# Attention inside a transformer layer on eight cores: softmax reciprocals broadcast in f32 without a bf16 copy, and a barrier ahead of attention

## The chip, the cores and the metric

The kernel runs on all 8 cores of one Trainium2 chip, cores 0 to 3 on one die and 4 to 7 on the other. Each core works on one of the 8 sequences of the batch and on nothing else; the cores exchange no data. The metric is the device time of the slowest core in microseconds.

## The reference

One layer: attention with a residual on a layer-normed input, then a linear map with low-rank updates and a residual, also on a layer-normed input. Each core has 2048 tokens of width 4096, 32 query heads and 8 key/value heads of width 128.

```python
x = x + attn(layernorm(x), Wq, Wk, Wv, Wo, cos, sin)
x = x + ffn(layernorm(x), W, bias, A, Bf, coeffs, scales)

# attn: each key/value head serves 4 query heads
q = rope((x @ Wq).reshape(b, s, 32, 128)); k = rope(x @ Wk); v = x @ Wv
scores  = einsum('bhqd,bhkd->bhqk', q, k) / sqrt(128)      # causal mask
weights = softmax(scores)
ctx     = einsum('bhqk,bhkd->bhqd', weights, v)
return ctx @ Wo

# ffn
out = x @ W.T + bias
upd = sum_e coeffs[e] * scales[e] * (x @ A[e].T) @ Bf[e].T
```

## The kernel before

Five programs, one for each engine, are written out by hand. Every engine runs its instructions in order; a helper `INC` counts a semaphore up when an instruction ends, `wge` makes an engine wait for a count, `W` makes one named engine wait for all counted so far. `bar` drains all engines and makes each wait for the others.

The stages run in this order, all with the width on the partitions and the tokens in the free dimension: constants (`p0`); for each half H of 1024 tokens a layer norm (`p_ln`), the projections of q, k and v (`p2`) and attention of that half's queries over all keys so far (`p3`); then the output projection (`p4`), two layer norms and the second linear map (`p6`). Before, there is a barrier after each `p3` and none between `p2` and `p3`.

`p2` makes 48 outputs of 128 rows: 32 q heads, spilled to memory as bf16 (`q_spill`), 8 k heads and 8 v heads kept on chip. For each q and k head it also finds the largest squared norm (L401, into `BND`). The k heads end before the v heads begin. In the v part TensorE transposes (L502) and ScalarE copies (L508) while VectorE has nothing left of `p2`.

`p3` first turns the norms into one bound for all scores: VectorE does 8 copies or maxima (L545, L547), 32 products (L553) and a reduction (L557) on single elements, ScalarE a root and a sign (L565, L567), TensorE a broadcast (L573), ScalarE a copy into `NEGB` (L579). Then it runs 32 blocks, for 16 pairs of heads and two groups jj of 512 queries. A block has `kcn` chunks of 128 keys: 4 and 8 in half 0, 12 and 16 in half 1, and the last four of each are masked. Per chunk, TensorE computes the scores of both heads (L681, L683), VectorE adds the mask where there is one (L702, L704), ScalarE takes the exponential into bf16 (L716), and TensorE adds the chunk to the denominators with a matrix of ones (L734, L735, PSUM columns 3072 to 4095) and to the context (L737, L738, PSUM columns 2048 to 3071). Scores run two chunks ahead.

At a block's end ScalarE copies the raw context out (L750, L751), and VectorE takes the reciprocals of the two denominators on one partition (L759, L760) into `ROWS` in f32, then casts both (L762, L763) into one row of `SQS` or `OSTG` in bf16. The context is scaled one block later by the tail: after the first two chunks' scores of block idx, the tail of block idx-2 is emitted. In it TensorE broadcasts the two reciprocals over 128 partitions into PSUM 2048 to 3071 (L605, L607), and VectorE copies these to `RBS` (L620, L621) and multiplies the context (L624, L625). In half 0 the result then goes to memory (L633, L635). VectorE's order at a block's start is thus: reciprocals and casts of block idx-1, tail of block idx-2, masks of block idx. TensorE's first L734 of a block waits for the casts of block idx-1, the context copies of block idx-1 and the `RBS` copies of block idx-2.

GpSimd loads each block's q (L658, L659) two blocks ahead. In either half the first two blocks' loads need only the first two spills of q and are issued once GpSimd has done its weight loads of `p2`. The f32 matrix of ones `ONESF`, one row of 128, is also used by `p_ln`, which broadcasts rows of f32 with it (L310 to L313).

Of the kernel before, what the change touches and what calls it, by code (L numbers as in the profile page):

```python
# [40 lines left out]
class B:  # L41
# [109 lines left out]
    def emit(self, me, eng):  # L151
        self.me = me
        self.eng = eng
        self.C = {k: 0 for k in SEM_NAMES}

        self.p0()
        self.bar()
        for H in (0, 1):
            self.p_ln(self.x_fm, lambda kc: self.arena(self.U1, kc), H,
                      dbg=self.dbg_ln1 if self.debug else None)  # L160
            if self.upto >= 2:
                self.p2(H)
            if self.upto >= 3:
                self.p3(H)
                self.bar()
            else:
                self.bar()
        if self.upto >= 2 and self.debug:
            self.p2_dbg()
            self.bar()  # L170
        if self.upto >= 4:
            self.p4()
            self.bar()
        if self.upto >= 5:
            for H in (0, 1):
                U = self.U1 if H == 0 else self.U2
                self.p_ln(self.xprime, lambda kc, U=U: self.arena(U, kc), H,
                          dbg=self.dbg_ln2 if self.debug else None)
        if self.upto >= 6:
            self.p6()  # L180
        self.bar()
        if self.on("sync"):
            self.eng.wait_ge(self.sems["out0"], self.C["out0"])
            self.eng.wait_ge(self.sems["out1"], self.C["out1"])
            self.eng.wait_ge(self.sems["dbg"], self.C["dbg"])
# [345 lines left out]
    def p3(self, H):  # L531
        on, INC = self.on, self.INC
        eng = self.eng
        PS, SCB, Q3, MSK, RBS = self.PS, self.SCB, self.Q3, self.MSK, self.RBS
        BND, NEGB, ROWS = self.BND, self.NEGB, self.ROWS
        RCB = self.SQS

        self.W("vector", "nrm")
        if on("vector"):
            self.wge("qsp", self.C["qsp"])  # L540
            i = None
            for kv in range(NKV):
                kslot = 64 + kv * 2 + H
# [47 lines left out]
        sc_tot = []  # L591
        pends = []

        def rcb_row(g, head):
            t = self.SQS if g % 2 == 0 else self.OSTG
            return t[0:1, head * 512:(head + 1) * 512]

        def emit_tail_pe(g):
            gi, h0, h1, jj = g
            if on("tensor"):  # L600
                self.wge("rc", base_rc + 2 * (gi + 1))
                self.wge("cev", base_cev + min(2 * (gi + 2), 2 * NH))
                if gi >= 1:
                    self.wge("rbe", base_rbe + 2 * gi)
                INC(eng.matmul(PS[:, 2048:2560], self.ONESR[0:1, :], rcb_row(gi, 0),  # L605
                               start=True, stop=True), "rb", 1)
                INC(eng.matmul(PS[:, 2560:3072], self.ONESR[0:1, :], rcb_row(gi, 1),  # L607
                               start=True, stop=True), "rb", 1)
            else:
                INC(None, "rb", 1)  # L610
                INC(None, "rb", 1)
# [30 lines left out]
        for hp in range(NH // 2):  # L642
            kv = hp // 2
            h0, h1 = 2 * hp, 2 * hp + 1
            for jj in range(2):
# [7 lines left out]
                if on("gpsimd"):  # L653
                    if idx >= 2:
                        self.wge("sc", sc_tot[idx - 2])
                    else:
                        self.wge("qsp", self.C["qsp"] - 16 * 30)
                    INC(eng.dma_start(qs0, self.q_spill[h0, :, q0:q0 + 512]), sq, 16)  # L658
                    INC(eng.dma_start(qs1, self.q_spill[h1, :, q0:q0 + 512]), sq, 16)  # L659
                else:  # L660
                    INC(None, sq, 16)
                    INC(None, sq, 16)
# [9 lines left out]
                def emit_scores(kc):  # L672
                    if on("tensor"):
                        if kc == 0:
                            self.wge(sq, base_q[p] + 32 * (idx // 2 + 1))
                            if idx == 0:
                                self.wge("ev2", self.C["ev2"])
                        if kc >= 2:
                            self.wge("exp", base_exp + (kc - 1))
                        lhsT = self.kfm(kv)[:, kc * 128:(kc + 1) * 128]  # L680
# [15 lines left out]
                for kc in range(kcn):  # L696
# [24 lines left out]
                    if on("tensor"):  # L721
                        self.wge("exp", base_exp + (kc + 1))
                        if kc == 0:
                            self.wge("rc", base_rc + 2 * idx)
                            self.wge("cev", base_cev + 2 * idx)
                            if idx >= 1:
                                self.wge("rbe", base_rbe + 2 * (idx - 1))
                            else:
                                self.wge("vev", self.C["vev"])
                                self.wge("nrm", self.C["nrm"])  # L730
                        st, sp = (kc == 0), (kc == kcn - 1)
                        e0 = SCB[:, (kc % 2) * 1024:(kc % 2) * 1024 + 512]
                        e1 = SCB[:, (kc % 2) * 1024 + 512:(kc % 2 + 1) * 1024]
# [18 lines left out]
                else:  # L752
                    INC(None, "cev", 1)
                    INC(None, "cev", 1)
                rc0 = ROWS[0:1, 0:512]
                rc1 = ROWS[0:1, 512:1024]
                if on("vector"):
                    self.wge("vdn", base_vdn + 2 * kcn)
                    INC(eng.reciprocal(rc0, PS[0:1, 3072:3584]), "chn", 1)  # L759
                    INC(eng.reciprocal(rc1, PS[0:1, 3584:4096]), "chn", 1)  # L760
                    self.wge("chn", self.C["chn"])
                    INC(eng.tensor_copy(rcb_row(idx, 0), rc0), "rc", 1)  # L762
                    INC(eng.tensor_copy(rcb_row(idx, 1), rc1), "rc", 1)  # L763
                else:
                    INC(None, "chn", 1)
                    INC(None, "chn", 1)
                    INC(None, "rc", 1)
                    INC(None, "rc", 1)
                pends.append((idx, h0, h1, jj))
# [260 lines left out]
```

## Time and profile before

| | us |
|---|---|
| median of 2 runs | 6090.76 |
| lowest and highest | 6077.15, 6104.36 |
| the profiled execution | 6069.31 |
| its span, slowest core (core 3) | 6067.8 |
| spans of the other cores | 6022.6 to 6056.3 |
| attention of half 0, half 1 on core 3, about | 727, 1073 |

The span is the time from the first to the last instruction of a core. All rows are of core 3. TensorE is busy for 77% of the span, VectorE for 33%, ScalarE for 21%. A line like L605 is line 605 of the kernel before. In a timeline, a matmul's start is measured and its end modelled: two matmuls that follow each other at the full clock start 0.22 us apart although each is shown with 0.38 us. The granted clock is that of TensorE, as a share of 2.4 GHz.

### The profile page before, as it was taken

Reading aid. Unit: us, or ns where it says so; the run is one execution under the profiler, and the core shown is the slowest. Engines: PE = TensorE matmul, PEld = TensorE weight load, DVE = VectorE, ACT = ScalarE, POOL = GpSimd, SP = SyncE. Lnnn points to the kernel's source line nnn. Section 1 sums busy time; section 2 is a strip of 40 time slices with the busy share of each in tenths; the row PEclk is TensorE's granted clock in tenths of the full one; section 3 lists DMA queues with packets and bytes.
Section 4 is the critical chain, followed back from the end, with each engine's and each line's share of the span. In section 5 each row is a group of like instructions: output and inputs, shape, how many; then the busy total and the mean of one; then the engine's idle time right before and its main releaser. Section 6 shows DMA issues by size and latency. Waiting matters only on the chain.

```text
span 6067.8 us, 50466 instructions; the slowest of 8 cores (6022.6 to 6067.8 us)
## 1 busy us (share of the span) xinstructions
PE 4660.8 (77%) x19656; PEld 1911.8 (32%) x19656; DVE 2019.1 (33%) x2001; ACT 1264.8 (21%) x1352; POOL 384.7 (6%) x366
## 2 busy tenths in 40 slices
PE   3399997454442999986666765899999446999999
PEld 0134443111110444432222222344444102444444
DVE  0644531666625454404444343000000172000000
ACT  4011112333332111124544544000000440000000
POOL 0001110000000111100000001000000000000000
PEclk6699998787765999998888888899999557999999
DMA  6278863000041888730000001666665532666665
GB/s 143 26 75 92 91 66 37 23 25 23 25 92 42 87 89 94 72 40 7 9 7 9 7 9 31 124 117 113 116 114 108 142 101 26 112 110 113 109 107 103
DMA packets 758102, 429.63 MB, mean 71 GB/s; under 512 B 685760, under 2 KB 693984, under 8 KB 757616
## 3 DMA queue, kind: packets, MB, share of 16 engines
q0 software_dynamic: 684144, 199.88, 32.8%
q1 hardware_dynamic: 73728, 226.53, 11.9%
q8 instruction: 164, 2.69, 0.2%
q14 instruction: 66, 0.54, 0.0%
HBM read 506.56 MB, written 92.27 MB: 99 GB/s over the span
## 4 chain that ended last, share of the span: by engine, by line
PE 67%; DVE 17%; DMA 8%; ACT 5%; issue 2%; POOL 0%; ACTq 0%; DVEq 0%; SPq 0%; POOLq 0%
PE PS L423 10%; PE PS L424 10%; PE PS L942 7%; PE PS L829 7%; PE PS L943 7%; PE PS L830 7%; DVE ROWS L759 4%; DVE ROWS L760 3%; PE PS L734 3%; DMA XST<-x_fm 3%; ACT SCB L716 2%; DMA WS<-wq 2%; PE PS L735 2%; PE PS L737 2%; DMA XST<-xprime 2%
## 5 line engine op out<-in xcount | busy, mean ns | idle before, releaser
L423 PE MATMUL PS<-U,WS 128*128 128x512 bf16 x3072 | 1180.1, 384 | 177.2 <-DVE U L333 150.7
L424 PE MATMUL PS<-U,WS 128*128 128x512 bf16 x3072 | 1178.5, 384 | 0.0
L716 ACT ACTIVATE SCB<-PS,NEGB 128x1024 bf16<-128x1024 f32 x640 | 708.5, 1116 | 919.8 <-PE PS L683 507.2
L829 PE MATMUL PS<-U,WS 128*128 128x512 bf16 x2048 | 777.7, 380 | 48.2 <-DMA WS<-wo 48.2
L942 PE MATMUL PS<-U,WS 128*128 128x512 bf16 x2048 | 777.7, 380 | 20.0 <-DMA BFT<-bf_r 20.0
L734 PE MATMUL PS<-SCB,ONES 128*128 128x512 bf16 x640 | 271.6, 424 | 678.2 <-ACT SCB L716 343.1
L943 PE MATMUL PS<-U,WS 128*128 128x512 bf16 x2048 | 777.7, 380 | 0.0
L830 PE MATMUL PS<-U,WS 128*128 128x512 bf16 x2048 | 777.6, 380 | 0.0
L702 DVE TENSOR_TENSOR PS<-PS,MSK 128x512 f32<-128x512 f32 x256 | 178.7, 698 | 971.2 <-PE PS L683 968.7
L423 PEld LDWEIGHTS PS<-U,WS 128*128 128x128 bf16 x3072 | 303.6, 99 | 577.4 <-issue 232.1
L424 PEld LDWEIGHTS PS<-U,WS 128*128 128x128 bf16 x3072 | 303.6, 99 | 360.3 <-issue 15.9
L260 ACT CAST U<-XST 128x1024 bf16<-128x1024 f32 x128 | 133.6, 1044 | 1158.3 <-DMA XST<-xprime 1022.4
L973 DVE SCALAR_TENSOR_TENSOR U<-PS,BIAS,XST 128x1024 f32<-128x1024 f32 x64 | 82.1, 1283 | 878.9 <-PE PS L953 713.6
L734 PEld LDWEIGHTS PS<-SCB,ONES 128*128 128x128 bf16 x640 | 66.1, 103 | 943.4 <-issue 942.3
L848 DVE TENSOR_TENSOR U<-PS,XST 128x1024 f32<-128x1024 f32 x64 | 78.4, 1225 | 855.5 <-PE PS L830 829.0
L829 PEld LDWEIGHTS PS<-U,WS 128*128 128x128 bf16 x2048 | 200.7, 98 | 291.6 <-issue 50.8
L401 DVE TENSOR_REDUCE BND<-PS 1x1 f32<-1x1024 f32 x80 | 97.0, 1212 | 584.2 <-PE PS L395 584.2
L942 PEld LDWEIGHTS PS<-U,WS 128*128 128x128 bf16 x2048 | 200.7, 98 | 262.9 <-issue 22.1
L943 PEld LDWEIGHTS PS<-U,WS 128*128 128x128 bf16 x2048 | 200.7, 98 | 242.5 <-issue 1.7
L830 PEld LDWEIGHTS PS<-U,WS 128*128 128x128 bf16 x2048 | 200.7, 98 | 242.4 <-issue 1.6
L460 ACT ACTIVATE OSTG<-XST 128x1024 bf16<-128x1024 f32 x64 | 67.6, 1057 | 987.1 <-DVE XST L446 987.1
L735 PE MATMUL PS<-SCB,ONES 128*128 128x512 bf16 x640 | 269.0, 420 | 0.0
(135 smaller groups left out, 4647.6 us busy)
## 6 DMA issues: line engine op xcount, KB each, us to landing
XST<-x_fm SPq DMA_DIRECT2D x128, 512.0 KB, 4.7
WS<-wq POOLq DMA_DIRECT2D x64, 1024.0 KB, 13.5
XST<-xprime SPq DMA_DIRECT2D x128, 512.0 KB, 4.3
WS<-wo POOLq DMA_DIRECT2D x32, 1024.0 KB, 16.1
xprime<-U SPq DMA_DIRECT2D x64, 512.0 KB, 3.5
WS<-wf POOLq DMA_DIRECT2D x32, 1024.0 KB, 16.9
out_fm<-U SPq DMA_DIRECT2D x64, 512.0 KB, 3.6
q_spill<-OSTG SPq DMA_DIRECT2D x64, 256.0 KB, 5.3
```

The lines of the kernel that those rows point to most:

```text
L423: eng.matmul(region[:, 0:512], lhsT, ln[:, 0:512], start=st, stop=sp)
L424: mmi = eng.matmul(region[:, 512:1024], lhsT, ln[:, 512:1024], start=st, stop=sp)
L702: eng.tensor_add(region(kc)[:, 0:512], region(kc)[:, 0:512], MSK[:, mi, :])
L716: INC(eng.activation(SCB[:, (kc % 2) * 1024:(kc % 2 + 1) * 1024], region(kc), AF.Exp, bias=NEGB[:, 0:1], scale=1.0), "exp", 1)
L734: eng.matmul(PS[:, 3072:3584], self.ONES2[:, :], e0, start=st, stop=sp)
L735: eng.matmul(PS[:, 3584:4096], self.ONES2[:, :], e1, start=st, stop=sp)
L759: INC(eng.reciprocal(rc0, PS[0:1, 3072:3584]), "chn", 1)
L760: INC(eng.reciprocal(rc1, PS[0:1, 3584:4096]), "chn", 1)
L829: eng.matmul(region[:, 0:512], lhsT, rhs[:, 0:512], start=st, stop=sp)
L830: mmi = eng.matmul(region[:, 512:1024], lhsT, rhs[:, 512:1024], start=st, stop=sp)
L942: eng.matmul(region[:, 0:512], lhsT, rhs[:, 0:512], start=st, stop=False)
L943: eng.matmul(region[:, 512:1024], lhsT, rhs[:, 512:1024], start=st, stop=False)
```

## The change

The two casts L762 and L763 go, with the wait between them and the reciprocals. The reciprocals of a block are written to one half of `ROWS`, by the block's parity, and the tail's broadcasts read them from there as f32, with `ONESF` in place of the bf16 ones `ONESR`. As a row of `ROWS` is used again two blocks later, the reciprocals of block idx wait for the broadcasts of block idx-2. A barrier of all engines comes between `p2` and `p3` in both halves. With it, the waits at the start of `p3` for q spills (`qsp`), rope results (`ev2`), v copies (`vev`) and norms (`nrm`) are taken out.

```diff
             if self.upto >= 2:
                 self.p2(H)
+            self.bar()
             if self.upto >= 3:
                 self.p3(H)
-                self.bar()
-            else:
                 self.bar()
...
         self.W("vector", "nrm")
         if on("vector"):
-            self.wge("qsp", self.C["qsp"])
...
-        def rcb_row(g, head):
-            t = self.SQS if g % 2 == 0 else self.OSTG
-            return t[0:1, head * 512:(head + 1) * 512]
+        def rec_row(g, head):
+            return ROWS[0:1, (g % 2) * 1024 + head * 512:(g % 2) * 1024 + (head + 1) * 512]
...
-                INC(eng.matmul(PS[:, 2048:2560], self.ONESR[0:1, :], rcb_row(gi, 0),
+                INC(eng.matmul(PS[:, 2048:2560], self.ONESF[0:1, :], rec_row(gi, 0),
                                start=True, stop=True), "rb", 1)
-                INC(eng.matmul(PS[:, 2560:3072], self.ONESR[0:1, :], rcb_row(gi, 1),
+                INC(eng.matmul(PS[:, 2560:3072], self.ONESF[0:1, :], rec_row(gi, 1),
                                start=True, stop=True), "rb", 1)
...
                     if idx >= 2:
                         self.wge("sc", sc_tot[idx - 2])
-                    else:
-                        self.wge("qsp", self.C["qsp"] - 16 * 30)
                     INC(eng.dma_start(qs0, self.q_spill[h0, :, q0:q0 + 512]), sq, 16)
...
-                            if idx == 0:
-                                self.wge("ev2", self.C["ev2"])
...
-                            else:
-                                self.wge("vev", self.C["vev"])
-                                self.wge("nrm", self.C["nrm"])
...
-                rc0 = ROWS[0:1, 0:512]
-                rc1 = ROWS[0:1, 512:1024]
                 if on("vector"):
                     self.wge("vdn", base_vdn + 2 * kcn)
-                    INC(eng.reciprocal(rc0, PS[0:1, 3072:3584]), "chn", 1)
-                    INC(eng.reciprocal(rc1, PS[0:1, 3584:4096]), "chn", 1)
-                    self.wge("chn", self.C["chn"])
-                    INC(eng.tensor_copy(rcb_row(idx, 0), rc0), "rc", 1)
-                    INC(eng.tensor_copy(rcb_row(idx, 1), rc1), "rc", 1)
+                    if idx >= 2:
+                        self.wge("rb", base_rb + 2 * (idx - 1))
+                    INC(eng.reciprocal(rec_row(idx, 0), PS[0:1, 3072:3584]), "rc", 1)
+                    INC(eng.reciprocal(rec_row(idx, 1), PS[0:1, 3584:4096]), "rc", 1)
```

## Rows read from the trace of the kernel before

**Rows 1.** Windows, the two attention stretches: length, then each engine's busy us, PEclk.

```profile
1009.00:1736.00 727.00, 350.63 (x1216) 119.26 (x1216) 458.46 (x510) 246.15 (x257) 31.96 (x60) 0.79 0.07 22
2702.00:3775.00 1073.00, 718.64 (x2752) 255.32 (x2752) 462.54 (x512) 528.26 (x513) 31.98 (x60) 0.87 0.02 8
```

**Rows 2.** Waits, whole span: who waited for whom, us, times, longest us.

```profile
PE PS L734 <- ACT SCB L716: 343.1, 196, 10.9
PE PS L734 <- DVE RBS L621: 307.9, 45, 7.0
```

**Rows 3.** Timeline of one block boundary: start us, us, instruction, idle before and releaser.

```profile
1114.10 3.35 DVE L759 RECIPROCAL ROWS<-PS 1x512 f32<-1x512 f32 x1 [2.54 <-PE PS L738]
...
1115.40 0.37 PE L605 MATMUL PS<-OSTG,ONESR 1*128 1x512 bf16 x1 [0.55 <-ACT U L751]
...
1115.62 0.37 PE L607 MATMUL PS<-OSTG,ONESR 1*128 1x512 bf16 x1
1117.37 3.28 DVE L760 RECIPROCAL ROWS<-PS 1x512 f32<-1x512 f32 x1
...
1121.43 0.67 DVE L620 CAST RBS<-PS 128x512 bf16<-128x512 f32 x1
...
1122.85 0.59 PE L734 MATMUL PS<-SCB,ONES 128*128 128x512 bf16 x1 [6.86 <-DVE RBS L621]
```

**Rows 4.** Groups by line, whole span, half of the casts: busy us, mean ns.

```profile
L762 DVE CAST SQS<-ROWS 1x512 bf16<-1x512 f32 x32 | 13.3, 415 | 3.3
L763 DVE CAST SQS<-ROWS 1x512 bf16<-1x512 f32 x32 | 13.0, 408 | 0.0
```

**Rows 5.** Timeline of the first layer norm: from the third broadcast to its reader.

```profile
166.61 1.91 PE L312 MATMUL PS<-XST,ONESF 1*128 1x512 f32 x2
...
170.32 1.01 ACT L319 COPY MR<-PS 128x1024 f32<-128x1024 f32 x1 [14.04 <-PE PS L313]
```

**Rows 6.** Timeline of the end of half 0: the last tail.

```profile
1734.04 0.58 PE L605 MATMUL PS<-OSTG,ONESR 1*128 1x512 bf16 x1 [6.44 <-DVE RBS L621]
...
1735.22 0.69 DVE L620 CAST RBS<-PS 128x512 bf16<-128x512 f32 x1 [0.40 <-PE PS L607]
```

**Rows 7.** Timeline of half 0: the softmax bound, from VectorE to the first scores.

```profile
869.44 0.56 DVE L545 COPY BND<-BND 1x1 f32<-1x1 f32 x8 [0.17 <-DVE BND L401]
...
872.52 0.17 DVE L557 TENSOR_REDUCE BND<-BND 1x1 f32<-1x32 f32 x1
...
1007.28 0.20 ACT L565 ACTIVATE BND<-BND 1x1 f32<-1x1 f32 x1
...
1009.07 0.59 PE L681 MATMUL PS<-Q,U 128*128 128x512 bf16 x1 [0.61 <-ACT NEGB L579]
```

**Rows 8.** Timeline across the barrier behind half 1.

```profile
3774.68 0.42 DVE L625 TENSOR_TENSOR U<-U,RBS 128x512 bf16<-128x512 bf16 x1
3775.28 0.33 SPq L839 DMA_DIRECT2D XST<-x_fm  x1
3775.74 0.54 POOL L801 DMA_DIRECT2D U<-ctx_sp  x1 [82.55 <-ACTq L138]
```

**Rows 9.** The line L659, the second q load of a block.

```profile
DMA to landing us min/median/max: 2.4/2.5/11.4
```

**Rows 10.** Groups by line, window of half 0, then of half 1: first scores matmul.

```profile
L681 PE MATMUL PS<-Q,U 128*128 128x512 bf16 x192 | 83.9, 437 | 0.6 <-ACT NEGB L579 0.6
...
L681 PE MATMUL PS<-Q,U 128*128 128x512 bf16 x448 | 182.6, 408 | 0.6 <-ACT NEGB L579 0.6
```

**Rows 11.** Timeline of TensorE in the q projection of half 0, behind two gaps.

```profile
277.57 0.38 PE L423 MATMUL PS<-U,WS 128*128 128x512 bf16 x1 [2.15 <-DMA WS<-wq]
...
297.32 0.59 PE L423 MATMUL PS<-U,WS 128*128 128x512 bf16 x1 [5.25 <-DVE MR L442]
297.70 0.63 PE L424 MATMUL PS<-U,WS 128*128 128x512 bf16 x1
...
303.24 0.40 PE L423 MATMUL PS<-U,WS 128*128 128x512 bf16 x1
```

More of the change, by code:

```diff
@@ L535, in p3 @@
         BND, NEGB, ROWS = self.BND, self.NEGB, self.ROWS
-        RCB = self.SQS
         self.W("vector", "nrm")
         if on("vector"):
-            self.wge("qsp", self.C["qsp"])
             i = None
@@ L754, in p3 @@
                     INC(None, "cev", 1)
-                rc0 = ROWS[0:1, 0:512]
-                rc1 = ROWS[0:1, 512:1024]
                 if on("vector"):
                     self.wge("vdn", base_vdn + 2 * kcn)
-                    INC(eng.reciprocal(rc0, PS[0:1, 3072:3584]), "chn", 1)
-                    INC(eng.reciprocal(rc1, PS[0:1, 3584:4096]), "chn", 1)
-                    self.wge("chn", self.C["chn"])
-                    INC(eng.tensor_copy(rcb_row(idx, 0), rc0), "rc", 1)
-                    INC(eng.tensor_copy(rcb_row(idx, 1), rc1), "rc", 1)
-                else:
-                    INC(None, "chn", 1)
-                    INC(None, "chn", 1)
+                    if idx >= 2:
+                        self.wge("rb", base_rb + 2 * (idx - 1))
+                    INC(eng.reciprocal(rec_row(idx, 0), PS[0:1, 3072:3584]), "rc", 1)
+                    INC(eng.reciprocal(rec_row(idx, 1), PS[0:1, 3584:4096]), "rc", 1)
+                else:
                     INC(None, "rc", 1)
```

## The prediction, made before the changed kernel was run

> **What bounds the kernel now.** I read the cores' spans first, then the windows, the waits, the groups by line, and last the timeline around single block boundaries. The change lies in the two attention halves, so only these matter. The windows [rows 1] give 727 us for half 0 and 1073 us for half 1. No engine is busy all the time in either: TensorE 351 and 719 us, VectorE 458 and 463 us, ScalarE 246 and 528 us, at a granted clock of 0.79 and 0.87. What sets the time is what TensorE waits for. The waits [rows 2] show two large ones ahead of L734, the first matmul on a fresh exponential: 343.1 us for ScalarE, 307.9 us for VectorE's L621, the latter in 45 waits of up to 7.0 us.
>
> The timeline of one boundary [rows 3] shows what L621 stands for. When a block's last matmul ends, VectorE starts two one-row reciprocals (3.35 and 3.28 us), then two one-row casts of their results (L762, L763), then the two evictions L620 and L621 that belong to the block before. Only then may TensorE overwrite the PSUM these read (L734 at 1122.85). TensorE's own part, the broadcast L605/L607, starts at 1115.40 and is over some 7 us before. So VectorE's chain is the path at the boundary. In the blocks that begin with masked chunks the release comes through the mask adds and an exponential, but these too queue on VectorE behind the same chain. There are 32 blocks in each half, 64 boundaries with the two half ends.
>
> **The change, part by part.**
>
> *The casts go.* Each is 415 and 408 ns [rows 4], on one partition; they overlap a little with their neighbours, so I take starts from the timeline [rows 3]. From L760's start (1117.37) to L620's start (1121.43) is 4.06 us. L760 takes 3.28 us, and without casts L620 could start about 3.21 us after it starts (an engine's next instruction starts here some 0.07 us before the record of the last one ends, as L760 follows L759: 1114.10 + 3.35 against 1117.37 leaves 0.08). Gain 4.06 - 3.21 = 0.85 us a boundary, 64 x 0.85 = 54 us. Nothing else covers it: TensorE is idle throughout.
>
> *The broadcasts read f32.* Attention shows none at this width; the layer norm does: two f32 broadcasts of one row of 512 (L312, L313, at the low clock) take from 166.61 to ScalarE's start at 170.32, 3.71 us [rows 5]. The bf16 pair starts 0.22 us apart at the full clock [rows 3]. As upper bound of the f32 pair I take 3.71 us, as lower bound the bf16 pair's 0.6 us; likely is about half the upper one, 1.9 us, since the clock is full there. At a boundary the pair starts at 1115.40 and would end by 1119.1 at worst; VectorE is in its reciprocals until 1120.6, so it costs nothing, with 1.5 us to spare. It starts when ScalarE's L751 ends, which is tied to the same last matmul as the reciprocals, so the margin is the same in every block. The new wait of the reciprocals on `rb` is for a broadcast issued a whole block earlier and is met. The Trainium skill, "FP8 and Floating Point Precision", section "TensorE Precision Notes", says that true FP32 takes four passes through the array; by it the pair would be 8 x 0.22 = 1.8 us at the full clock, and hidden as well.
>
> At each half's end the cover is gone: the last tail starts when VectorE is done and all wait for it. There the bf16 pair takes from 1734.04 to L620 at 1735.22, 1.18 us [rows 6], and the f32 pair at the low clock 3.71 us: +2.5 us, twice, +5 us.
>
> *The barrier before attention.* Now VectorE's work for the softmax bound runs during the V projection: 869.44 to 872.69, 3.25 us [rows 7], over 130 us before it is needed. Behind a barrier it comes after the last V copy. A barrier costs 0.2 to 0.6 us from the last engine's end to the others' next issue [rows 8]; I take 0.25. Then 3.25 us, one handover of 0.1, and the rest of the chain as before (L565 at 1007.28 to L681 at 1009.07, 1.79 us). Added: 3.6 us a half, +7 us. The first q loads, until now issued ahead, start behind the barrier too: POOL at 0.65 us after the last engine's end [rows 8], two issues of 0.54, landing 2.5 us after the second issue starts [rows 9]: about 3.7 to 4.2 us, against 5.4 us of the bound chain, hidden. Queued behind these on POOL are only later q loads. The waits taken out cost nothing by themselves; SP's `qsp` wait at the end of the projection is for spills long landed.
>
> *Sum.* -54 + 5 + 7 = -42 us against the profiled execution's 6069.3 us: 6027. That execution is 21.5 us below the median of the runs, 6090.8 us; so -42 us from there, 6049 us.
>
> **What the clock may do.** It is the largest unknown. Each block begins at the low clock: L681's mean is 437 ns in half 0 and 408 in half 1 [rows 10]. A matmul's record is 0.38 us at the full clock and 0.63 at the low one [rows 11]. So (437 - 380)/250 = 23% of the 1152 matmuls of half 0 and 11% of the 2688 of half 1 ran low (the other five lines of a chunk lie near L681), 560 in all, nearly 9 a block. Low ones start 0.42 us apart (14 of them from 297.32 to 303.24 [rows 11]), full ones 0.22: 0.21 us lost each, about 118 us in all. The change shortens TensorE's idle gap before L734: from 6.86 us by 0.85 and by 1.3 for the longer broadcast, to about 4.7 us. Would the clock then stay up? In the projection a gap of 2.15 us left the matmul after it at 0.38; one of 5.25 us was followed by 14 low ones [rows 11]. 4.7 us is nearer to the second, so I take no gain, and keep -118 us as the bound below. The bound above: if every block had the 14 low matmuls of that case instead of 9, 5 x 0.21 x 64 = +67 us.
>
> **The rivals.**
>
> *Clock held.* If the shorter gap keeps the full clock in every block: -42 - 118 = -160 us, 5931 us, 2.6% faster; in half of them 5990. For it: the gap shrinks by a third. Against it: the 5.25 us case, and gaps of the masked blocks, which are longer. The Trainium skill, "TensorE: Matmul & The Clock Gate", section "HAM oscillation", says that waits between bursts of matmuls make each burst start at the low clock, and only long ones do; by it shortening a gap can pay more than its own length. The low starts here agree with it.
>
> *Longer low spells.* The instants at which the level changes are not tied to the blocks, so a shift of the blocks may lengthen them; at the bound -42 + 67 = +25, 6116 us, slower than before. It decides from 42/(0.21 x 64) = 3 more low matmuls in a block on average. For it: spells of 14 occur. Against it: nothing selects the long ones.
>
> *f32 broadcasts not hidden.* They must take over 5.2 us a pair (1115.40 to 1120.6). At twice the layer norm's 3.71 us, 2.2 us more in 62 blocks: -42 + 136 + 7 = +101 us, 6192 us. The row speaks against it.
>
> *q loads late.* The longest landing is 11.4 us [rows 9], beside weight loads: 0.65 + 0.54 + 11.4 - 5.4 = 7 us a half, +14: 6063 us. No weights are in flight behind the barrier.
>
> *The change doesn't pay.* If the blocks were paced by something else and the casts only filled a wait, -54 falls away: +12 us, 6103 us. The chain of [rows 3], without a gap on VectorE, speaks against it.
>
> **How the numbers follow.** Forecast 0.68; q late 0.10; longer low spells 0.08; doesn't pay 0.06; clock held 0.06; not hidden 0.02. Predicted: 6049 us, 0.7% below before. The range of 6005 to 6100 takes in the forecast with the executions' own scatter (6077 to 6104 us before), q late, half of the clock's bounds and most of the case of no gain. What this kernel's measurement can tell from no change is 2%, 122 us. Faster by more: the clock held in most blocks, 0.05. Slower by more: 0.02. Within: 0.93.
>
> **What would show it.** No L762/L763; L620 about 3.2 us after L760's start; TensorE's gap before L734 about 4.7 us; f32 broadcasts of some 1.9 us a pair that end before L620 starts, half 0 near 703 us and half 1 near 1048 us, each from its first scores; VectorE's bound work between the last V copy and the first scores, 3.6 us. L681's mean near 437 and 408 would confirm that the clock is unchanged. Wrong would be: L620 waiting for a broadcast, or these means well off.

## The result and the profile after

| | before | after |
|---|---|---|
| executions, us, without the disturbed | 6070.5 to 6104.4 (8) | 6031.1 to 6060.9 (10) |
| ratio of the two | | 0.9932, 95% interval 0.9915 to 0.9949 |
| profiled execution, its span, us | 6069.3, 6067.8 | 6034.8, 6033.2 |
| last V transpose to first scores | 2.4 | 5.9 |
| half 0, first scores to last scaling | 729.5 | 716.7 |
| half 1 | 1073.8 | 1045.7 |
| low matmuls in half 0, half 1 | 284, 339 | 341.5, 328.5 |

The change makes the kernel 0.7% faster, some 41 us of 6080. (About half of all executions, of either kernel, were disturbed on one die or both and took 3 to 12% longer; with them the median before is 6180.87 us and after 6047.87, a difference that the change did not make.) The last four lines are medians over the cores whose matmul records are complete, worked out from the trace. A low matmul is one of the six chunk lines whose record is over 0.5 us; the total is 1152 in half 0 and 2688 in half 1. These four numbers are the yardstick for everything below: what lies ahead of the first scores alone differs by 23 to 33 us between the cores of one execution (they start at 976 to 1009 us before, at 984 to 1007 after), the halves by 1 to 3.

In the code after, the reciprocals are L748 and L749, the broadcasts L601 and L603, the evictions L616 and L617, and the first matmul on a fresh exponential L723. The same windows as [rows 1], on the slowest core (length, then busy us of TensorE, weight loads, VectorE, ScalarE and GpSimd, each with its count, granted clock, DMA share, GB/s):

```profile
1006.00:1725.00 719.00, 408.60 (x1282) 141.12 (x1282) 433.71 (x448) 246.45 (x259) 32.07 (x60) 0.80 0.07 23
2685.00:3732.00 1047.00, 757.35 (x2818) 273.36 (x2818) 436.73 (x448) 528.49 (x515) 32.07 (x60) 0.89 0.03 8
```

VectorE has 62 and 64 instructions and some 25 us less in a half: the casts. TensorE has 66 records and 58 and 39 us more: some 45 us a half are the longer f32 broadcasts, which run where it would be idle, the rest in half 0 is longer records of chunk matmuls. The halves are shorter by 8 and 26 us in these rough cuts, by 12.8 and 28.1 us when measured from first scores to last scaling. The two halves did not gain alike. The waits (who waited for whom, us, times, longest) beside [rows 2]:

```profile
PE PS L723 <- ACT SCB L708: 306.4, 197, 8.4
PE PS L723 <- DVE RBS L617: 208.4, 45, 4.7
```

The wait for the evictions is 99.5 us shorter, though only 54 us of casts went: 45 such waits shrink by 0.85 us for the casts, and by some 1.3 us that the longer broadcasts now fill (97 us in all), and the second part gains nothing. Ahead of the blocks of 4 chunks, which begin with a masked one, TensorE's wait is longer in both kernels, 10.5 us before and 8.3 after. One block boundary, beside [rows 3] (timeline, core 1: start, us, instruction, idle before it and its releaser):

```profile
2822.85 3.35 DVE L748 RECIPROCAL ROWS<-PS 1x512 f32<-1x512 f32 x1 [2.60 <-PE PS L727]
...
2824.09 1.09 PE L601 MATMUL PS<-ROWS,ONESF 1*128 1x512 f32 x2 [0.55 <-ACT U L740]
...
2825.02 1.02 PE L603 MATMUL PS<-ROWS,ONESF 1*128 1x512 f32 x2
...
2826.12 3.28 DVE L749 RECIPROCAL ROWS<-PS 1x512 f32<-1x512 f32 x1
2829.33 0.61 DVE L616 CAST RBS<-PS 128x512 bf16<-128x512 f32 x1
2829.88 0.66 DVE L617 CAST RBS<-PS 128x512 bf16<-128x512 f32 x1
...
2830.69 0.58 PE L723 MATMUL PS<-SCB,ONES 128*128 128x512 bf16 x1 [4.65 <-DVE RBS L617]
```

From L749's start to L616's it is 3.21 us, against 4.06 in [rows 3]. The f32 broadcasts take 1.95 us together and are over 3.3 us before L616 starts. L616 waits for nothing: VectorE's chain from L748 to L723 is still the path. It is 7.84 us now, and was 8.75.

The start of half 0, beside [rows 7] (timeline, slowest core): the bound work has moved behind the barrier.

```profile
1001.56 0.50 ACT L507 CAST U<-PS 128x128 bf16<-128x128 f32 x2 [0.30 <-PE PS L501]
1002.30 0.56 DVE L542 COPY BND<-BND 1x1 f32<-1x1 f32 x8 [139.95 <-ACTq L138]
1002.71 0.57 POOL L652 DMA_DIRECT2D Q<-q_spill  x1 [41.05 <-ACTq L138]
...
1005.38 0.17 DVE L554 TENSOR_REDUCE BND<-BND 1x1 f32<-1x32 f32 x1
...
1007.34 0.59 PE L673 MATMUL PS<-Q,U 128*128 128x512 bf16 x1 [0.50 <-ACT NEGB L576]
```

The barrier itself costs 0.24 us from ScalarE's last copy (1002.06) to VectorE's first one; then come 3.25 us of scalar work on one element, L542 to L554, that [rows 7] shows 130 us earlier. TensorE is released by the bound (L576), not by the q load, which was issued at 1002.71.

The end of half 0, beside [rows 6] (timeline, core 3), where nothing lies beside the broadcasts:

```profile
1708.53 2.04 PE L601 MATMUL PS<-ROWS,ONESF 1*128 1x512 f32 x2 [3.72 <-DVE RBS L617]
...
1710.37 1.91 PE L603 MATMUL PS<-ROWS,ONESF 1*128 1x512 f32 x2
...
1712.80 0.69 DVE L616 CAST RBS<-PS 128x512 bf16<-128x512 f32 x1 [3.49 <-PE PS L603]
```

From L601 to L616 it is 4.27 us at the low clock, against 1.18 before: +3.1 us. At the end of half 1 it is 3.92 (3720.00 to 3723.92), +2.7.

Last the clock, by the mean record of a chunk's lines in half 0. The scores line of before is in [rows 10], 437 ns; its context line (groups by line, core 3, busy us and mean ns):

```profile
L737 PE MATMUL PS<-SCB,U 128*128 128x512 bf16 x192 | 83.4, 434 | 0.0
```

and the two lines after, on the slowest core:

```profile
L673 PE MATMUL PS<-Q,U 128*128 128x512 bf16 x192 | 85.3, 444 | 0.5 <-ACT NEGB L576 0.5
L726 PE MATMUL PS<-SCB,U 128*128 128x512 bf16 x192 | 88.8, 463 | 0.0
```

The scores matmul hardly shows it (437 to 444), the context matmul does (434 to 463): more of half 0 runs at the low clock than before.

### The profile page after: what moved, and what is told of

Read it like the earlier page. It is cut to its first block, busy times and chain, and to the rows that moved or that the text cites. A ratio compares the mean times of both kernels' runs of the same rounds, so it can differ in the third digit from the quotient of the medians.

```text
span 6033.2 us, 50608 instructions; the slowest of 8 cores (6005.6 to 6033.2 us)
## 1 busy us (share of the span) xinstructions
PE 4755.1 (79%) x19784; PEld 1950.1 (32%) x19784; DVE 1967.2 (33%) x1873; ACT 1264.5 (21%) x1352; POOL 385.4 (6%) x366
## 3 DMA queue, kind: packets, MB, share of 16 engines
q1 hardware_dynamic: 73728, 226.53, 12.8%
## 4 chain that ended last, share of the span: by engine, by line
PE 66%; DVE 13%; DMA 9%; ACT 6%; issue 5%; POOL 0%; ACTq 0%; DVEq 0%; SPq 0%; POOLq 0%
PE PS L422 10%; PE PS L423 10%; PE PS L813 7%; PE PS L814 7%; PE PS L926 7%; PE PS L927 7%; DVE ROWS L748 3%; PE PS L723 3%; DMA WS<-wq 3%; DMA XST<-x_fm 3%; ACT SCB L708 3%; DMA XST<-xprime 2%; PE PS L724 2%; PE PS L726 2%; PE PS L727 2%
## 5 line engine op out<-in xcount | busy, mean ns | idle before, releaser
L723 PE MATMUL PS<-SCB,ONES 128*128 128x512 bf16 x640 | 270.7, 423 | 548.1 <-ACT SCB L708 306.4
L723 PEld LDWEIGHTS PS<-SCB,ONES 128*128 128x128 bf16 x640 | 66.0, 103 | 828.8 <-issue 827.7
```

What stands on the lines that cost most here:

```text
L723: eng.matmul(PS[:, 3072:3584], self.ONES2[:, :], e0, start=st, stop=sp)
```

## The experiments

All are changes to the kernel after, except e2 and e7, which change the kernel before. All compute the whole reference. This table has the yardstick for each; the expectations stand as written before each ran. "Chain" is the time from the first reciprocal's start to the first eviction's start at a boundary, against before.

| kernel | chain | gap | half 0 | half 1 | low, half 0 | low, half 1 | ratio to before (95%) |
|---|---|---|---|---|---|---|---|
| before | 0 | 2.4 | 729.5 | 1073.8 | 284 | 339 | 1 |
| after | -0.85 | 5.9 | 716.7 | 1045.7 | 341.5 | 328.5 | 0.9932 (0.9915 to 0.9949) |
| e1, no barrier | -0.85 | 2.4 | 716.1 | 1046.4 | 336 | 333 | 0.9959 (0.9914 to 1.0003) |
| e2, barrier alone | 0 | 6.1 | 731.0 | 1072.5 | 294 | 341.5 | 1.0054 (1.0013 to 1.0096) |
| e3, bf16 reciprocal | -0.85 | 6.0 | 714.0 | 1043.4 | 342 | 330 | 0.9966 (0.9927 to 1.0005) |
| e4, more broadcasts | -0.85 | 5.9 | 724.9 | 1100.5 | 338 | 326 | 1.0046 (1.0014 to 1.0078) |
| e7, casts twice | +0.68 | 2.5 | 762.7 | 1098.9 | 339.5 | 353 | 1.0107 (1.0049 to 1.0165) |
| e11, one copy | -0.24 | 6.1 | 726.9 | 1065.6 | 296 | 339 | none |
| e8, filled gap | -0.85 | 6.0 | 708.7 | 991.8 | 344.5 | 69 | 0.983 |
| e5, direct reciprocal | | 5.9 | 679.3 | 1005.6 | 375 | 312.5 | 0.9792 (0.9746 to 0.9839) |
| e6, denominators out | | 6.0 | 605.9 | 809.2 | 350.5 | 14 | 0.943 |
| e10, mask by matmul | | 6.1 | 389.6 | 765.6 | 10.5 | 13.5 | 0.892 |

Gap, halves and counts are as in the first table. Ratios without an interval rest on one or two executions.

**e1, no barrier.** The waits at the start of attention come back for the barrier, with two differences: GpSimd's is for all spills of q and not the first two, and VectorE's for the spills stays out. The rest of the change stays.

```
-            self.bar()
...
+                    else:
+                        self.wge("qsp", self.C["qsp"])
...
+                            if idx == 0:
+                                self.wge("ev2", self.C["ev2"])
...
+                            else:
+                                self.wge("vev", self.C["vev"])
+                                self.wge("nrm", self.C["nrm"])
```

> The changed kernel without its new barrier, with the waits at the start of attention put back; casts gone and f32 broadcasts as in the changed kernel. Chain theory (the time is VectorE's chain at each block boundary, the barrier only uncovers the bound's work): first scores about 2.5 us after the last V transpose instead of 6.0, halves unchanged at 717 and 1046 us, so some 7 us less than the changed kernel, ratio to before about 0.992. Rival (the barrier shifts the blocks and is what took back the missing 12 us of half 0): half 0 falls to about 705 us, ratio about 0.990.

Measured: the gap is back at 2.4 us and the halves are those of after, 716.1 and 1046.4 us. So the barrier costs 3.5 us a half ahead of the first scores, and changes nothing inside. Its 7 us are too few for the ratio: the intervals of e1 and after overlap.

**e2, barrier alone.** The kernel before with the barrier added, its precise waits kept.

```
+            self.bar()
```

> The kernel before with a barrier added between projection and attention, all else unchanged, casts and bf16 broadcasts kept. Chain theory: first scores 6.0 instead of 2.5 us after the last V transpose, halves unchanged at 729 and 1073 us, +7 us in all, ratio 1.001. Rival (the barrier disturbs more, by q loads that start late or by projection weights that come later): first scores over 8 us after the last transpose or another stage longer, ratio over 1.003.

Measured: the gap grows to 6.1 us, the halves stay (731.0 and 1072.5). The ratio, 1.0054, is more than the 7 us (0.1%) explain; in the profiled execution the excess lies in the projections of half 0 on cores 4 and 5, whose first scores start at 1053 and 1059 us, against 983 and 976 before (the granted clock in these projections is 0.90 on core 5 and 0.98 on core 1). The barrier comes behind these projections. The two runs give the barrier nearly the same price from both sides, 3.5 to 3.9 us a half.

**e3, bf16 reciprocal.** The reciprocal writes the bf16 row itself, so the casts are gone and the broadcasts are bf16, as before.

```
         def rec_row(g, head):
-            return ROWS[0:1, (g % 2) * 1024 + head * 512:(g % 2) * 1024 + (head + 1) * 512]
+            t = self.SQS if g % 2 == 0 else self.OSTG
+            return t[0:1, head * 512:(head + 1) * 512]
...
-                INC(eng.matmul(PS[:, 2048:2560], self.ONESF[0:1, :], rec_row(gi, 0),
+                INC(eng.matmul(PS[:, 2048:2560], self.ONESR[0:1, :], rec_row(gi, 0),
...
```

> The changed kernel with the reciprocals written as bf16 rows and broadcast by the bf16 ones: casts gone as in the change, but broadcasts as short as before; the barrier stays. Chain theory: VectorE's chain is as in the changed kernel, so half 1 stays near 1046 us and each half ends 2.5 us sooner; TensorE's gap before the first denominator matmul is about 6.0 instead of 4.7 us. Clock theory for half 0 (the missing 12 us are low-clock matmuls, set by where the blocks fall): the number of low matmuls in half 0 moves with the gap or not, and half 0's time moves by 0.21 us for each. Rival (the f32 broadcasts themselves cost in half 0): half 0 near 704 us with an unchanged number of low matmuls.

Measured: halves of 714.0 and 1043.4 us, 2.7 and 2.3 below after, all of it at the half ends. The period of a block of 4, 8, 12 and 16 chunks is 16.62, 27.68, 29.55 and 35.20 us, against 16.62, 27.67, 29.53 and 35.20 after. Inside the blocks the f32 broadcasts cost nothing. The low matmuls are those of after (342 and 330), with TensorE idle for 1.3 us longer at each boundary: what broadcasts fill of the gap makes no difference to the clock.

**e4, more broadcasts.** Three more f32 one-row matmuls at each boundary, to see when the cover ends and whether work on one row holds the clock.

```
+                for rep in range(2):
+                    eng.matmul(PS[:, 2048:2560], self.ONESF[0:1, :], rec_row(gi, 0),
+                               start=True, stop=True)
+                eng.matmul(PS[:, 2560:3072], self.ONESF[0:1, :], rec_row(gi, 1),
+                           start=True, stop=True)
```

> The changed kernel with three more f32 broadcasts in each tail, repeats of the same two into the same place, so that TensorE's idle gap before the first denominator matmul falls from about 4.7 to about 2.1 us in three of four blocks; VectorE's chain is the same. If one-row matmuls hold the clock up: low matmuls fall from about 340 and 320 to under 150 in each half, and some 60 to 100 us go, ratio about 0.980. If the clock doesn't count them or the gap is still too long: low matmuls and halves as in the changed kernel, ratio 0.993. If a tail starts at the low clock it takes 8.5 us, longer than its cover of 5.2: then up to 3 us more in such a block.

Measured: half 0 +8.2 us, half 1 +54.8 us against after. The low matmuls hardly move (338 and 326). The block periods in half 0 are those of after (16.64 and 27.65 us), and 5.1 of its 8.2 us are the last tail, which has no cover; in half 1 they grow by 1.8 and 1.3 us. One boundary of half 1 tells why (timeline, core 4; the first row holds two instructions):

```profile
2795.22 3.35 DVE L753 RECIPROCAL ROWS<-PS 1x512 f32<-1x512 f32 x1 [2.61 <-PE PS L732]
...
2796.46 1.95 PE L602 MATMUL PS<-ROWS,ONESF 1*128 1x512 f32 x4 [0.55 <-ACT U L745]
2798.25 1.60 PE L604 MATMUL PS<-ROWS,ONESF 1*128 1x512 f32 x2
2798.49 3.28 DVE L754 RECIPROCAL ROWS<-PS 1x512 f32<-1x512 f32 x1
2799.65 1.91 PE L606 MATMUL PS<-ROWS,ONESF 1*128 1x512 f32 x2
2801.35 1.91 PE L608 MATMUL PS<-ROWS,ONESF 1*128 1x512 f32 x2
2803.44 0.69 DVE L621 CAST RBS<-PS 128x512 bf16<-128x512 f32 x1 [1.66 <-PE PS L608]
```

TensorE works without a pause from 2796.46, and still its instructions go from 1.02 us to 1.91: the clock fell to its lower level (1.2 GHz) while TensorE ran one-row matmuls back to back; the granted clock is 1.00 in the 6 us before them and 0.65 over them. With that five of them outlast VectorE's reciprocals, and L621 waits 1.66 us for L608. In half 0 the last of them are shorter (L608 takes 1.4 us on average, 2.1 in half 1), and L621 waits 3.7 us for them in all, against 57.5 in half 1. This is the rival "f32 broadcasts not hidden", made to happen: it needs 2.5 times the work of the change.

**e7, casts twice.** The kernel before, with each cast done twice: two more casts in the chain.

```
+                    eng.tensor_copy(self.WS[0:1, 0, 0:4, :], rc0)
+                    eng.tensor_copy(self.WS[0:1, 0, 4:8, :], rc1)
                     INC(eng.tensor_copy(rcb_row(idx, 0), rc0), "rc", 1)
                     INC(eng.tensor_copy(rcb_row(idx, 1), rc1), "rc", 1)
```

> The kernel before with two more one-row casts at each block's end, the same as L762 and L763 but into an unused place; no barrier. Chain theory: VectorE's chain is 0.68 us longer at each of 64 boundaries, +43 us if the low-clock matmuls stay at 282 and 335 a half; each one more or fewer moves that by 0.21 us. Both halves' block periods grow by 0.68 us on average before that. Rival (part of the casts is covered, as half 0's gain of 12 instead of 24 us would say): half 0 grows by about half of 22 us with an unchanged number of low matmuls.

Measured: the two extra casts take 0.68 us from start to start. The halves grow by 33.2 and 25.1 us. 32 x 0.68 = 21.8 us of each is the chain. The rest, 11.4 and 3.3, is again low matmuls: 55.5 and 14 more, at 0.21 us 11.7 and 2.9. A longer chain also raises the count in half 0. The rival, casts that are partly covered, would have had half 0 grow by 11 us.

**e11, one copy.** The kernel after, with one one-row copy ahead of its reciprocals, so that the chain lies between that of after and that of before.

```
+                    eng.tensor_copy(self.SQS[0:1, (idx % 2) * 512:(idx % 2) * 512 + 512],
+                                    PS[0:1, 3072:3584])
                     INC(eng.reciprocal(rec_row(idx, 0), PS[0:1, 3072:3584]), "rc", 1)
```

> The changed kernel with one more VectorE instruction ahead of each block's reciprocals, a one-row copy of 512 out of PSUM into an unused place, some 0.60 us. VectorE's chain is then 0.25 us shorter than before the change, where the changed kernel's is 0.85 us shorter. Chain theory with the clock: half 0 takes 729 - 32 x 0.25 + 2.5 = 723.5 us plus 0.21 us for each low matmul above 283, half 1 1073.5 - 8 + 2.5 = 1068 us plus 0.21 us for each above 337; each within 3 us. The counts themselves are not foretold, except that they need not lie between those of the two kernels. Rival (half 0's missing 12 us is a cost that grows evenly with the chain): half 0 about 14 us over the changed kernel's, 731, whatever the counts.

Measured on core 1 alone, since in the only execution cores 2 and 3 took 2.7 times as long for half 0 and 3.7 times for half 1 (26 ms in all), and cores 4 to 7 took some 150 us longer outside the halves. Its chain is 0.24 us shorter than before's: 7.09 us (2852.84 to 2859.93) against 7.33 in [rows 3]. Half 0 is 726.9 us with 296 low matmuls, half 1 1065.6 with 339. The same row of arithmetic: 729.5 - 32 x 0.24 + 2.5 + 12 x 0.21 = 726.8; for half 1 it gives 1068.6, 3 us too much. So a quarter of the shortening brings a fifth of the additional low matmuls; but three other cores of that execution with whole records have 276, 306 and 279, as wide as before's own 281 to 299, so that the count did not clearly rise here.

**e8, filled gap.** The kernel e3, with 18 full-height bf16 matmuls (K as stationary, q as moving operand, results unused) ahead of the broadcasts at each boundary.

```
+                if fill is not None:
+                    for r in range(18):
+                        c = 2048 + (r % 2) * 512
+                        eng.matmul(PS[:, c:c + 512], fill[0], fill[1], start=True, stop=True)
```

> The changed kernel with bf16 reciprocals and bf16 broadcasts, and ahead of the two broadcasts of each tail 18 more matmuls of full height, 128x512 bf16, whose results nobody reads; they fill TensorE's idle time while VectorE takes the reciprocals. VectorE's chain is the same. Clock theory: matmuls of full height hold the clock where one-row matmuls did not; in three of four blocks TensorE then idles under 2.5 us. Low matmuls fall from about 340 and 327 to under 150 and 80; at 0.21 us each some 80 to 100 us go, ratio about 0.980. Rival (the low clock costs nothing, since ScalarE or VectorE paces those chunks): fewer low matmuls, but halves within 10 us of 714 and 1043.

Measured: half 1 falls from e3's 1043.4 to 991.8 us and its low matmuls from 330 to 69, half 0 from 714.0 to 708.7 with the count unchanged in the median (344.5, the cores from 278 to 382). Window of half 1 on core 1, after first, then e8:

```profile
2680.00:3727.00 1047.00, 749.23 (x2785) 270.41 (x2782) 436.77 (x448) 520.55 (x507) 42.72 (x81) 0.89 0.04 11
```

```profile
2692.00:3684.00 992.00, 769.48 (x3275) 288.59 (x3273) 436.67 (x448) 523.82 (x509) 40.77 (x77) 0.98 0.03 11
```

The granted clock is 0.98 instead of 0.89. TensorE does 540 useless matmuls more and is done sooner. Against e3, which has the same chain, it is 51.6 us for 261 low matmuls fewer, 0.20 us each. This settles the price of a low matmul, and that the clock, not only the chain, sets the time in half 1.

The filling is not the same in half 0. It takes 4 us of each wait and leaves 1.9 to 2.0 us ahead of blocks of 8, 12 and 16 chunks, but 5.7 us ahead of every block of 4, where the first mask adds and an exponential follow VectorE's chain. Two boundaries of half 0 (timeline, core 1):

```profile
1106.99 0.38 PE L729 MATMUL PS<-SCB,ONES 128*128 128x512 bf16 x1 [1.82 <-DVE RBS L623]
...
1134.08 0.59 PE L729 MATMUL PS<-SCB,ONES 128*128 128x512 bf16 x1 [5.69 <-ACT SCB L714]
```

By blocks the low matmuls of half 0 go from 10.9 to 7.3 in a block of 8 and from 10.1 to 13.8 in a block of 4, so the two cancel. Why those of 4 have more than without the filling is not explained.

**e5, direct reciprocal.** The ones matrix already leaves the denominators on all 128 partitions, so the reciprocal can be taken there, and broadcast and eviction go.

```
-                    INC(eng.reciprocal(rec_row(idx, 0), PS[0:1, 3072:3584]), "rc", 1)
-                    INC(eng.reciprocal(rec_row(idx, 1), PS[0:1, 3584:4096]), "rc", 1)
+                    self.wge("nmm", self.C["nmm"])
+                    INC(eng.reciprocal(RBS[:, 0, :], PS[:, 3072:3584]), "rc", 1)
+                    INC(eng.reciprocal(RBS[:, 1, :], PS[:, 3584:4096]), "rc", 1)
```

> The denominators already stand on all 128 partitions, as they come from a matrix of ones. This kernel takes the reciprocals there (128x512 in place of 1x512), into RBS as bf16, and multiplies the same block's context at once: no casts, no broadcasts, no RBS copies; barrier as in the changed kernel. If a reciprocal costs by its row length alone (3.3 us as on one partition), VectorE's chain ahead of the first denominator matmul loses the two RBS copies, 1.27 us a boundary: 64 x 1.27 = 81 us less than the changed kernel, and each half's end is shorter by about 5 us; ratio about 0.978, give or take 0.21 us for each low matmul more or less. If it costs more on 128 partitions, no gain.

Measured: 0.9792, halves of 679.3 and 1005.6 us. One boundary (timeline, core 1):

```profile
2791.10 3.36 DVE L717 RECIPROCAL RBS<-PS 128x512 bf16<-128x512 f32 x1 [2.61 <-PE PS L697]
...
2794.38 3.29 DVE L718 RECIPROCAL RBS<-PS 128x512 bf16<-128x512 f32 x1
...
2797.92 0.58 PE L693 MATMUL PS<-SCB,ONES 128*128 128x512 bf16 x1 [6.13 <-DVE RBS L718]
```

A reciprocal of 128 rows of 512 costs 3.36 us, of one row 3.35. The chain to the first matmul is 6.82 us against 7.84 after: 1.02 us a boundary (1.27 expected), 33 us a half, and the tail at the half end (6.5 us) is gone. That is 39 us; measured are 37.4 and 40.1, with 33 more low matmuls in half 0 (+7 us) and 16 fewer in half 1 (-3). With these the sum is 32 and 42 us, so it misses half 0 by 5 us and half 1 by 2.

**e6, denominators out.** The denominators are copied out of PSUM to SBUF at once, so that PSUM is free after two copies, and the reciprocals run under the next block.

```
+                INC(eng.reciprocal(RBS[:, head, :], dn), "rbe", 1)
...
-                    INC(eng.reciprocal(rec_row(idx, 0), PS[0:1, 3072:3584]), "rc", 1)
-                    INC(eng.reciprocal(rec_row(idx, 1), PS[0:1, 3584:4096]), "rc", 1)
...
+                    INC(eng.tensor_copy(DEN[:, dp:dp + 512], PS[:, 3072:3584]), "rc", 1)
+                    INC(eng.tensor_copy(DEN[:, dp + 512:dp + 1024], PS[:, 3584:4096]), "rc", 1)
```

> The reciprocals leave the path: at a block's end VectorE only copies the denominators of all partitions to SBUF (two copies of 128x512, 1.3 us), so that TensorE may go on; the reciprocals (128x512, bf16 out) and the context's scaling follow while the next block runs, ahead of its masks in blocks of 8 to 16 chunks and between the masks in those of 4. Chain theory: TensorE's wait falls from about 7.5 us after its last matmul to about 2.7, some 5 us less in 48 blocks and 1 to 2 in 16, 250 to 270 us; with the short gap the low matmuls of the 48 blocks go too, up to 100 us more. Ratio 0.940 to 0.955. Rival (something else paces the blocks): under 100 us.

Measured: halves of 605.9 and 809.2 us, an execution of 5734 us. One boundary (timeline, core 0):

```profile
2807.51 0.69 DVE L731 COPY XST<-PS 128x512 f32<-128x512 f32 x1 [2.61 <-PE PS L710]
...
2808.11 0.68 DVE L732 COPY XST<-PS 128x512 f32<-128x512 f32 x1
...
2808.97 3.35 DVE L604 RECIPROCAL RBS<-XST 128x512 bf16<-128x512 f32 x1 [0.17 <-DVE XST L732]
2809.87 0.38 PE L706 MATMUL PS<-SCB,ONES 128*128 128x512 bf16 x1 [1.68 <-ACT SCB L693]
```

The reciprocal is still there and as long as ever, but the next matmul starts 0.90 us into it: 2.36 us after the chain's start instead of 7.84. TensorE now waits for the exponential (L693), and only 14 of half 1's matmuls are low. In half 1, 5.48 x 32 = 175 us and 314 x 0.21 = 66 us make 241 us; measured are 236.5 less than after. In half 0 it is 111 us less, 3.5 a boundary, with as many low matmuls as ever (350.5). There TensorE still waits 3.4 us ahead of a block of 4 chunks and 4.0 us inside each block: the masks share VectorE with the reciprocals, which led to e10.

**e10, mask by matmul.** On top of e6 the causal mask is added by TensorE, in bf16 and with the identity, into the PSUM of the scores, instead of by eight VectorE operations a block. The reciprocals now stand ahead of the chunks in every block; in e6 they stood between the masks in blocks of 4.

```
+                        if kc >= diag0:
...
+                            eng.matmul(region(kc)[:, 0:512], lhsT, qs0, start=True, stop=False)
+                            eng.matmul(region(kc)[:, 512:1024], lhsT, qs1, start=True, stop=False)
+                            INC(eng.matmul(region(kc)[:, 0:512], idb, mk,
+                                           start=False, stop=True), "sc", 1)
+                            INC(eng.matmul(region(kc)[:, 512:1024], idb, mk,
+                                           start=False, stop=True), "sc", 1)
...
-                    isdiag = kc >= diag0
+                    isdiag = False
```

> As the kernel whose denominators are copied out, and the causal mask is added by TensorE, a matmul of a bf16 unit matrix with the mask into the scores, instead of by VectorE (L702, L704 before). The two mask adds of 0.69 us on VectorE and one handover go from each masked chunk's path, for two matmuls of 0.22 us. Half 0 is 605 us and half 1 809 us without this. If VectorE paces half 0's blocks (masks and reciprocals share it, 14 us of work in a block of 15): half 0 falls by 90 to 150 us, half 1 by 60 to 100 us (4 chunks of 2 us more each in 32 blocks, down to the plain chunk's pace); ratio 0.900 to 0.920. If ScalarE or TensorE paces them: half 0 by under 50 us.

Measured: 5442 us, with before at 6098 us on that chip (in another execution 6161), 0.892: the best kernel of this study. Windows of the two halves, core 4:

```profile
1018.00:1412.00 394.00, 317.56 (x1406) 131.68 (x1407) 281.69 (x192) 244.32 (x259) 35.37 (x62) 0.98 0.15 46
2360.00:3150.00 790.00, 679.61 (x2990) 273.11 (x2988) 286.32 (x234) 531.85 (x525) 39.81 (x75) 0.98 0.04 13
```

In both TensorE is the busiest engine now, at a clock of 0.98. Half 0 is 216 us shorter than in e6, where 90 to 150 were expected, and half 1 only 44, where 60 to 100 were: the masks are off VectorE, and in half 0 the low matmuls go with them, from 350 to about 10, which are 71 us at 0.21. The other 145 us of half 0 are 4.5 us a block, near the 8 x 0.69 = 5.5 us of mask operations.

## Why the prediction was right, and where it was not

Predicted were -42 us and 6049 us; measured are -0.68%, some 41 us, and 6047.9. The mechanism and three of the four steps hold. One step failed, the clock's, which was put at nothing and measured some 10 us, and the total hides it.

*The casts.* Right: 0.85 us a boundary (3.21 for 4.06 us from the second reciprocal's start to the eviction). e7 adds two casts, which are 21.8 us of what each half grows by, e11 takes back a part: the chain goes into the time one to one in both directions. The rival "the change doesn't pay" falls with these.

*The f32 broadcasts.* Right: 1.95 us a pair, predicted 1.9, and hidden inside the blocks (e3). The Trainium skill, "FP8 and Floating Point Precision", section "TensorE Precision Notes", gives four passes, from which the prediction had an estimate of 1.8 us by the full-clock spacing of [rows 3]: the trace agrees. At the half ends +3.1 and +2.7 us where 2.5 was said. e4 shows how far the rival "not hidden" was: five such instructions at a boundary, with a clock that falls during them, are enough.

*The barrier.* Right: 3.6 us predicted, 3.5 by after's gap and by e1, 3.7 to 3.9 by e2. The q loads (issued at 0.65 us behind ScalarE's end) are hidden behind the bound chain, so "q loads late" falls.

*The clock.* Here the step "4.7 us is nearer to the second, so I take no gain" failed as to its term, and with it "would confirm that the clock is unchanged". The gap was as predicted (4.65 us; 8.3 ahead of blocks of 4), no block held the clock (each has 6 low matmuls or more), but the number of low matmuls did not stay: +57 in half 0, -10 in half 1. At 0.21 us that is +12.1 and -2.2, +10 us in all, where the prediction had 0. By halves:

- half 0: 729.5 - 27.2 + 2.5 + 12.1 = 716.9; measured 716.7
- half 1: 1073.8 - 27.2 + 2.5 - 2.2 = 1046.9; measured 1045.7

The same holds block by block. Blocks of 4, 8, 12 and 16 chunks have 1.3, 1.8 and 0.8 more and 1.4 fewer low matmuls; 0.85 us less 0.21 for each gives 0.58, 0.47, 0.68 and 1.15 us, and the mean periods shrink by 0.55, 0.49, 0.77 and 1.10. Within one kernel, blocks of equal length differ by 0.17 to 0.18 us for each low matmul (before, a straight line through all blocks of a length), so 0.21 is rather the upper end of the price.

So the halves and the gaps give 54 - 5 - 10 - 7 = 32 us less, not 42; measured are 12.8 + 28.1 - 7 = 34 us. The profiled executions differ by 34.5 us, the ratio over many by 41. The 7 us between are within what the executions in the result's table scatter (30 to 34 us), and no run shows where they lie; that the total met the forecast is in part luck. Half 0 near 703 us was also wrong by a slip in the reading: [rows 1] give 727 us for a window cut by eye, and 729.5 is the half. The sign "L681's mean near 437 and 408" did not serve: it came out at 444 and 407, since most of the additional low matmuls fell on the other lines of a chunk. The rival "longer low spells" is the true one in its mechanism, with 57/32 = 1.8 more low matmuls a block in half 0 and none in half 1, where 3 more in a block on average would have made the kernel slower.

*Why the count changes* stays open. Not by the barrier: e1 has 336 and 333 without it, e2 294 and 341.5 with it. Not by the broadcasts: bf16 (e3) and f32 (after) give 342 and 341.5, three more (e4) 338. It goes with the chain. In half 1 the count rises with it: 312.5 in e5, whose chain is the shortest, 328.5 at -0.85 us, 339 at -0.24 and at 0, 353 at +0.68. In half 0 it is lowest at the chain of before: 375, 341.5, 276 to 306, 284, 339.5 in the same order. What makes half 0 so was not found. The blocks one by one show where to look. Before, the count wanders: ten blocks of 4 in a row on core 1 have 6, 13, 9, 13, 8, 7, 13, 9, 7 and 6. After, nearly all blocks of 4 have 10 and of 8 have 11, and in half 1 there are two patterns: 8 in a block of 12 and 12 in one of 16 on three cores, 14 and 7 on three others, in the same execution of the same program. So the kernel's instructions alone do not set the count. It looks like a matter of how the blocks' period falls against the instants at which the clock changes, which a small change of the period can shift; that is argued, no run tests it. What is shown is the price: 0.21 us a low matmul, from [rows 11], closes the sums of after, e3 and e7 to 1.3 us in both halves, and that of e8's half 1 to 3 us. In half 0 e8 is 6 us off and e5 5 us.

*The gap and its length.* "By 1.3 for the longer broadcast" counted the broadcasts as work that keeps the clock. No run shows that they do. The Trainium skill, "TensorE: Matmul & The Clock Gate", section "HAM oscillation", says that waits between bursts make each burst start low; e6's half 1 and both halves of e10, where no wait in a block is much over 2 us, agree with it (14 low matmuls of 2688 in half 1), and so does e8's half 1. Shortening the wait from 6.9 to 4.7 us brought none of that.

## What to carry to other kernels

Follow the chain that frees the buffer that the next matmul needs, and price only what is on it: there two casts of 0.4 us count in full, and 1.3 us of longer matmul counts nothing. Then ask whether the chain has to be there at all: copying the denominators out first (e6, 6%) and moving the mask to TensorE as well (e10, 11%) gave 8 and 16 times what the change gave; at 0.21 us a low matmul, a seventh and a fifth of what the halves lost is the clock's. Count low matmuls by half beside the times; without that count a change of 10 us in a half looks like a wrong price of something else.

## What the runs showed of the hardware

- A reciprocal on VectorE takes 3.35 us for one row of 512 and 3.36 us for 128 rows of 512 (e5), 4.9 times a copy of 128 rows (0.69 us, e6). A row of 1024 in the layer norm takes 6.54 us (L305 of before): its time goes by the row's length and not by the number of rows. The Trainium skill, "VectorE: DVE Perf Modes", section "First, the fixed hardware budget", says that it is an iterative division with a repeat count of 8; it gives no time, and the 4.9 times of a copy is what is measured here.
- One-row matmuls, in f32 and back to back for 6.8 us, did not keep TensorE's clock up: it fell during them in half 1 of e4, and the count of low matmuls afterwards was as without them (326 for 328.5). Full-height bf16 ones, 18 for 4 us, did in half 1, where they left waits of 2 us (69 for 330 low), and did not in half 0 as a whole, where every second wait was still 5.7 us.
- With TensorE busy for 78 to 82% of half 0 and 84 to 87% of half 1, on all 8 cores at once, the granted clock was 0.97 to 0.99 (e10, profiled execution).
